# Fetching and splitting a stage's first operands in the stage before: a five-stage expert kernel on one core

## What is computed

```python
def L0_cond(x, t):                      # 1 shared and 8 routed experts, top 2
    shared = (silu(x @ sw1.T) * (x @ sw3.T)) @ sw2.T
    s = sigmoid(x @ router_w.T + (t @ router_t_w.T)[:, None])
    combine = normalized gates of the top 2 of s + router_bias
    routed = sum_e combine[e] * (gelu(x @ rw1[e].T) @ rw2[e].T)
    return (shared + routed) / 3

def L0_ffn(h):                          # one of 8 experts for each batch
    sel = argmax(softmax(gelu(h[:, -1] @ Wp1 + bp1) @ Wp2 + bp2))
    z = gelu(h @ W1[sel] + b1[sel]) @ W2[sel] + b2[sel]
    return h + 0.3 * (z @ Wo + bo)

def L1_cond(x, token_ids, first):       # 16 experts by a hash of the token id
    d = shift(x, first) - x             # the token before, in each batch
    y = sum over a token's expert of relu(xk @ w_key[e])**2 @ w_value[e]     # xk = x + d * maa_k
    return sigmoid((x + d * maa_r) @ w_recept) * y

def L1_ffn(x):                          # a recurrence over the 32 batches, state c: 128 x 512
    for xt in x:
        f, i = sigmoid(xt @ wf.T + c @ uf.T + bf), sigmoid(xt @ wi.T + c @ ui.T + bi)
        c = f * c + i * tanh(xt @ wc.T + c @ uc.T + bc)
    return tanh(x @ wo.T + c @ uo.T + bo)

x = x + L0_ffn(L0_cond(x, cond))
x = x + L1_ffn(L1_cond(x, token_ids, cond))
```

## Time and profile before

| | |
|---|---|
| runs of the kernel before | 2596.1 us median of 3 (2594.2 to 2601.7) |
| the profiled execution | 2597.6 us, span 2595.9 us |
| instructions | 40713 |
| mean granted clock of PE | 0.98 |
| busy, share of the span | PE 95%, PE weight loads 79%, DVE 44%, ACT 35%, POOL 21% |
| read from and written to device memory | 541.9 and 161.6 MB |

### The profile page before, as it was taken

One profiled execution on the slowest core, in us unless ns is written; L12 is line 12 of the kernel. 1 busy time (PEld: TensorE's weight loads), 2 busy tenths in 40 slices (PEclk: granted clock), 3 DMA queues, 4 the chain that ended last, 5 costly groups with the idle time before them and its releaser, 6 DMA issues. The chain is left out here.

```text
span 2595.9 us, 40713 instructions
## 1 busy us (share of the span) xinstructions
PE 2476.0 (95%) x12551; PEld 2058.9 (79%) x12553; DVE 1141.7 (44%) x1746; ACT 900.9 (35%) x1451; POOL 555.3 (21%) x498
## 2 busy tenths in 40 slices
PE   8999999998999599999999969999969999999999
PEld 4788888877888488888888859999958888888876
DVE  4655455432333144343434336666733323332356
ACT  2333333324555222222222236666632222222233
POOL 1100000002222166657656520000001111111000
PEclk9999999998999799999999989999989999999999
DMA  7699898877444643364344246666631111111035
GB/s 289 219 329 324 296 335 306 316 281 277 141 142 145 245 155 114 114 239 128 105 152 148 89 180 245 224 238 223 242 132 33 33 28 28 33 33 29 19 105 170
DMA packets 137648, 446.60 MB, mean 172 GB/s; under 512 B 30578, under 2 KB 33074, under 8 KB 118368
## 3 DMA queue, kind: packets, MB, share of 16 engines
q1 hardware_dynamic: 109904, 342.78, 37.5%
q0 software_dynamic: 18736, 60.80, 7.7%
q10 hardware_dynamic: 8928, 41.98, 4.2%
HBM read 541.93 MB, written 161.58 MB: 271 GB/s over the span
## 5 line engine op out<-in xcount | busy, mean ns | idle before, releaser
L93 PE MATMUL s_g<-wx_hi,s_x_hi 128*128 128x512 f32 x512 | 206.7, 404 | 6.6 <-DVE s_x_lo L1931 4.0
L95 PE MATMUL s_g<-wx_hi,s_x_lo 128*128 128x512 f32 x512 | 201.8, 394 | 0.0
L94 PE MATMUL s_g<-wx_lo,s_x_hi 128*128 128x512 f32 x512 | 201.2, 393 | 0.0
L1665 DVE TENSOR_TENSOR s_w_lo<-s_w_raw,s_w_hi 128x1024 fp32r<-128x1024 f32 x128 | 151.0, 1222 | 68.0 <-ACT s_w_hi L1617 66.4
L93 PE MATMUL s_g<-s_w_hi,s_c_hi 128*128 128x512 f32 x384 | 152.4, 397 | 0.0
L93 PE MATMUL s_h_ps<-s_x_hi,s_w_hi 128*128 128x256 f32 x512 | 145.8, 285 | 6.4 <-DVE s_w_lo L1665 6.4
L95 PE MATMUL s_g<-s_w_hi,s_c_lo 128*128 128x512 f32 x384 | 149.8, 390 | 0.0
L94 PE MATMUL s_g<-s_w_lo,s_c_hi 128*128 128x512 f32 x384 | 149.4, 389 | 0.0
L95 PE MATMUL s_h_ps<-s_x_hi,s_w_lo 128*128 128x256 f32 x512 | 145.6, 284 | 0.0
L94 PE MATMUL s_h_ps<-s_x_lo,s_w_hi 128*128 128x256 f32 x512 | 145.6, 284 | 0.0
L1832 POOL DMA_INDIRECT s_y<-mid_hash_out,s_rec x32 | 31.4, 982 | 484.9 <-DMA s_rec<-mid_rec 480.1
(11 more groups left out here) (355 smaller groups left out, 6850.3 us busy)
## 6 DMA issues: line engine op xcount, KB each, us to landing
s_half<-mid_w ACTq DMA_DIRECT2D x128, 2048.0 KB
s_w_raw<-in_w SPq DMA_DIRECT2D x64, 512.0 KB, 6.1
mid_w<-s_x_grp SPq DMA_DIRECT2D x32, 1024.0 KB, 5.3
mid_w<-s_pool_b SPq DMA_DIRECT2D x32, 1024.0 KB, 4.9
s_w_raw<-in_w1h SPq DMA_DIRECT2D x16, 2048.0 KB, 8.3
s_w_raw<-in_w2h SPq DMA_DIRECT2D x16, 2048.0 KB, 7.5
mid_routed<-s_o_sb SPq DMA_DIRECT2D x72, 256.0 KB, 2.4
s_w<-mid_rw SPq DMA_DIRECT2D x8, 2048.0 KB, 19.8
```

The lines of the kernel that those rows point to most:

```text
L93: pe.matmul(out, a_hi, w_hi, start=first, stop=False, skip_group_check=True)
L94: pe.matmul(out, a_hi, w_lo, start=False, stop=False, skip_group_check=True)
L95: return pe.matmul(out, a_lo, w_hi, start=False, stop=last, skip_group_check=True)
L1665: dve.tensor_tensor(lo[:, c], raw[:, c], hi[:, c], ALU.subtract).then_inc(S[name + "_lo"], 1)
```

## The change

At all four places where a stage follows another, something that the later one needs first is fetched, or fetched and split, in the earlier one:

- Stage 1 no longer splits rw in parts. SP loads experts 0 to 4 raw, 1 MB each, into the place of their low halves; ACT writes the high halves (`routed_hi`), DVE overwrites the raw with the low. DVE gets twelve small operations in `places`, which note at which of the tiles 40, 48, 56, 64 and 72 the experts 3 and 5 are done (`unused_by`).
- Stage 2 loads experts 5 to 7 raw and splits them in tiles 2 to 7 (`late_hi`, `late_lo`). At tile 36 SP loads what stage 4's first batch needs; at each of the five tiles named, `load_first` loads the first w1 and w2 into `half` under a condition. It doesn't wait for its last output stores; POOL does in stage 4.
- Stage 4 loads and splits stage 5's first w1 (`load_hashed`, `hashed_hi`, `hashed_lo`), does the last batch's `mix` on DVE (`last_mix`), and leaves its last stores to stage 5.
- Stage 5 loads, in its last expert, the state weights, the first state and the first rows of stage 6, and splits the first two (`unit_hi`, `unit_lo`, `turn_state`, `state_hi`, `state_lo`).
- Stage 6 starts with the state products of batch 0 (`first_c_part`) and leaves them out of the pipeline.

Buffers move to other places so that what is loaded ahead doesn't meet what is still used. The core of the diff:

```diff
 stage_shared
-        PARTS = [("rw", 0), ("rw", 1)] + [(w, k) for w in ("w1", "w2") for k in range(DC)]
+        PARTS = [(w, k) for w in ("w1", "w2") for k in range(DC)]
...
             for e in range(EARLY):
-                row = sp.value_load(keep["order"][0:1, 0, e:e + 1], min_val=0, max_val=ER - 1)
-                sp.dma_start(keep["w"][:, bass.ds(row, 1)].bitcast(FP32),
-                             d["rw"][bass.ds(row, 1)].rearrange("o p l s n -> p o l s n")).then_inc(S[f"rw_in{e}"], 16)
+                sp.dma_start(keep["w_raw"][e][:, :, 1], raw_experts[:, e]).then_inc(S[f"rw_in{e}"], 16)
...
+            def routed_hi(e):
+                act.wait_ge(S["gu"], G * HC)
+                act.wait_ge(S[f"rw_in{e}"], 16)
+                act.activation(keep["w"][:, e, :, 0], keep["w_raw"][e][:, :, 1], ACT.Copy).then_inc(S["rw_hi"], 1)
             def o_out(g):
                 for m in range(TG):
+                    if g == G - 1:
+                        routed_hi(m)
+                        if m == TG - 1:
+                            routed_hi(EARLY - 1)
...
+                for n, last_expert in enumerate((3, 5)):
+                    for k, tiles in enumerate(CHECKED):
+                        op(dve.tensor_scalar(reached[:, n, k:k + 1], end[0:1, last_expert:last_expert + 1], float(tiles),
+                                             None, ALU.is_le))
...
+            for e in range(EARLY):
+                dve.wait_ge(S["rw_hi"], e + 1)
+                dve.tensor_tensor(keep["w"][:, e, :, 1], keep["w_raw"][e][:, :, 1], keep["w"][:, e, :, 0],
+                                  ALU.subtract)
 stage_routed
             for e in range(EARLY, ER):
+                sp.dma_start(w_raw[e][:, :, 1], raw_experts[:, e]).then_inc(S[f"w_in{e}"], 16)
...
+                if i == CHECKED[0] - 4:
+                    sp.wait_ge(S["ordered"], 1)
+                    for dst, src in (("bo", "bo"), ("maa_k", "maa_k"), ("maa_r", "maa_r")):
+                        sp.dma_start(keep["s4_" + dst][:], ins[src].partition_broadcast(P)).then_inc(S["s4_params_in"], 16)
...
+                if i + 1 in CHECKED:
+                    for layer in range(2):
+                        load_first(layer, CHECKED.index(i + 1))
...
+            def load_first(layer, n):
+
+                unused = sp.value_load(keep["unused_by"][0:1, layer, n:n + 1], min_val=0, max_val=1) > 0
+                e = sp.value_load(order[0:1, 0, 0:1], min_val=0, max_val=ER - 1)
+                s = sp.value_load(table[0:1, layer, 0:1], min_val=0, max_val=NW - 1)
+                sp.wait_ge(S["mm2"], CHECKED[n])
+                for k, name in enumerate((("s4_w1_in0", "s4_w1_in1"), ("s4_w2_in00", "s4_w2_in10"))[layer]):
+                    sp.dma_start(half[:, bass.ds(s, 1), 2 * k:2 * k + 2].bitcast(FP32),
+                                 d["w"][bass.ds(2 * e + 2 + layer, 1), :, 2 * k:2 * k + 2].rearrange("o p k s n -> p o k s n"),
+                                 cond=unused).then_inc(S[name], 16)
             straight(RT, [(0, store), (0, load)])
-            for n in range(NI):
-                sp.wait_ge(S[f"o_out{n}"], 16 * RT // NI)
...
+            def late_hi(i):
+                n = i - LATE_AT
+                if 0 <= n < len(LATE):
+                    e, layer = LATE[n]
+                    act.wait_ge(S[f"w_in{e}"], 16)
+                    act.activation(w[:, e, layer, 0], w_raw[e][:, layer, 1], ACT.Copy).then_inc(S["w_hi"], 1)
...
-            straight(RT, [(2, gelu), (1, x_hi_), (3, o_copy), (2, h_hi), (3, wo_hi), (0, choose)])
+            straight(RT, [(2, gelu), (1, x_hi_), (3, o_copy), (2, h_hi), (0, late_hi), (3, wo_hi), (0, choose)])
 stage_ffn
+            def load_hashed(i, n, turn):
+                if isinstance(i, int) and i == NB - 1:
+                    sp.wait_ge(S["mm2"], NB)
+                    sp.dma_start(keep["w1_raw"][:], ins["w1h"][0]).then_inc(S["hashed_in"], 16)
...
             sp.wait_ge(S["x1_out"], 16 * NB)
-            sp.wait_ge(S["r_out"], 16 * NB)
...
             def gather(i, n, turn):
+                if isinstance(i, int) and i == 0:
+                    for m in range(4):
+                        pool.wait_ge(R[f"o_out{m}"], 16 * RT // 4)
...
+            def hashed_hi(i, n, turn):
+                if isinstance(i, int) and i == NB - 1:
+                    act.wait_ge(S["hashed_in"], 16)
+                    for c in range(DC):
+                        act.activation(keep["w1_hi"][:, c], keep["w1_raw"][:, c], ACT.Copy).then_inc(S["hashed_hi"], 1)
...
-                (1, h_lo(0)), (2, x1_), (1, h_lo(1)), (3, part_lo(xr_lo, tz_ps, xr_hi, "xr_hi", "xr_lo")),
+                (1, h_lo(0)), (2, x1_), (1, h_lo(1)), (3, last_mix),
+                (3, part_lo(xr_lo, tz_ps, xr_hi, "xr_hi", "xr_lo")), (3, hashed_lo),
 stage_hashed
+            def load_ahead(e):
+                if isinstance(e, int) and e == EH - 1:
+                    sp.wait_ge(F["r_out"], 16 * NB)
+                    sp.dma_start(staged[:], ins["gate_w"][0:NST].rearrange("u p n -> p u n")).then_inc(S["u_in"], 16)
+                    sp.dma_start(first_rec[:], d["rec"][0]).then_inc(S["rec_in"], 16)
+                    for m in range(2):
+                        sp.wait_ge(S[f"tx{m}"], EH)
+                    sp.dma_start(first_c[:], ins["in_c"].partition_broadcast(P)).then_inc(S["c_in"], 16)
+                    sp.dma_start(first_r[:], d["r"][0]).then_inc(S["r_in"], 16)
...
+                (2, g_hi), (2, out(1)), (1, w2(0, 2)), (1, relu(0)), (1, w2(2, 3)), (1, relu(1)), (1, h_hi(0)), (1, w2(3, 4)),
+                (1, unit_hi(0, 1)), (1, relu(2)), (1, h_hi(1)), (1, unit_hi(1, 2)), (1, relu(3)), (1, h_hi(2)),
+                (1, h_hi(3)), (1, unit_hi(2, 4)), (1, state_hi), (1, unit_hi(4, UNITS)), (0, x_hi_(0)), (0, x_hi_(1)),
+                (0, w1(0, 4)), (1, out(0))])
 stage_recurrent
+            def first_c_part():
+                for g in range(NG):
+                    for k in range(DC):
+                        product(pe, g_ps[0][g][:], (c_hi[:, k], c_lo[:, k]), (state_w(0, g, k), state_w(1, g, k)),
+                                k == 0, False)
...
             def c_part(i, n, turn):
-                pe.wait_ge(S["c_lo"], i + 1)
+                if isinstance(i, int) and i == 0:
+                    return
...
-            turn_c(0)
+            first_c_part()
```

More of the change, by code:

```diff
@@ L32 @@
 AHEAD_BYTES = 4 * D * 4
+UNITS = 6
+STATE_BYTES = (2 * D + 2 * UNITS * HS + 2 * D + D) * 4
 EPS = 1e-9
@@ new lines, in stage_ffn @@
+        keep["w1_lo"], keep["w1_hi"], keep["w1_raw"] = ahead("w1_lo", 1), ahead("w1_hi", 2), ahead("w1_raw", 3, FP32)
+        right = lambda n, s, t=FP32: ctx.enter_context(nc.sbuf_tensor("s4_" + n, s, t, side="right"))
+        right("half", [P, HALF_BYTES // 4])
+        half = keep["half"]
+        r = right("r", [P, D])
+        y_hi = right("y_hi", [P, DC, P], FP32R)
+        y_lo = right("y_lo", [P, DC, P], FP32R)
+        h_pre = right("h_pre", [P, 2, D])
+        h = right("h", [P, 2, D])
@@ new lines, in stage_ffn @@
+        ht_hi = right("ht_hi", [P, HC, P], FP32R)
+        ht_lo = right("ht_lo", [P, HC, P], FP32R)
+        z = right("z", [P, D])
+        z_hi = right("z_hi", [P, DC, P], FP32R)
+        z_lo = right("z_lo", [P, DC, P], FP32R)
+        b1 = right("b1", [P, HS])
+        b2 = right("b2", [P, D])
+        base = right("base", [P, 2, D])
+        y_part = right("y_part", [P, D])
+        right("first", [P, (CHOICE_BYTES + FIRST_BYTES) // 4])
+        shared, bo, maa_k, maa_r = (keep["s4_" + n] for n in ("shared", "bo", "maa_k", "maa_r"))
@@ L1648, in stage, with unit_hi, state_hi @@
                     wait_for(act, S[f"o_out{m}"], e * 16)
-                    act.activation(o_sb[:, m], o_ps[m][:], ACT.Copy).then_inc(S[f"o_ready{m}"], 1)
+                    act.activation(o_sb[m][:], o_ps[m][:], ACT.Copy).then_inc(S[f"o_ready{m}"], 1)
                 return stage
+            def unit_hi(first, end):
+                def stage(e):
+                    if isinstance(e, int) and e == EH - 1:
+                        for n in range(first, end):
+                            if n < 2:
+                                act.wait_ge(S["u_in"], 16)
+                                act.wait_ge(S["w1_lo"], (EH - done["w1"]) * DC)
+                            else:
+                                act.wait_ge(S["h_ps"], EH * NQ)
+                            if n >= NST:
+                                act.wait_ge(S["u_again_in"], 16)
+                            act.activation(u[:, n, 0], staged[:, n % NST], ACT.Copy).then_inc(S["u_hi"], 1)
+                return stage
+            def state_hi(e):
+                if isinstance(e, int) and e == EH - 1:
+                    act.wait_ge(S["c_turned"], 1)
+                    act.wait_ge(S["h_ps"], EH * NQ)
+                    act.activation(keep["c_hi"][:], tx_ps[0][:], ACT.Copy).then_inc(S["c_hi"], 1)
```

(14 more changed lines are left out.)

367 lines of the change are left out of this document (209 added, 158 removed).

## The result

The changed kernel takes 2584.5 us (median of 7 runs, 2580.9 to 2587.3) against 2598.3 us (median of 7, 2594.2 to 2601.7): a ratio of 0.9942, 95% interval 0.9931 to 0.9953, so 0.6% faster. The direction was forecast, the size was not: 14 us instead of 41, outside the range of 2536 to 2574 us. The profiled execution has a span of 2579.9 us, 16.0 less than the 2595.9 of before.

What follows compares the result with a forecast made beforehand. TensorE, busy 95% of the span, was taken as the bound, so only its standstills and the half clock after them could be won. Terms summed to 40.6 us: 2597.6 to 2557.0, stated as 2556 against the median, range 2536 to 2574.

Steps and rivals of the forecast that it cites:

- Stage 1: Stage 1: twelve small VectorE operations ahead of the scan delay the product that frees gate bank 0, -1.7 us.
- Seam 1 to 2: Between stages 1 and 2: TensorE restarts 0.5 us after VectorE's last subtraction, near 582.7, +1.0 us.
- Stage 2: Stage 2: late expert splits -2.4 us, stall at tile 4 gone +9.8, load burst after tile 39 stalling tile 44 -14.3.
- Seam 2 to 4: Between stages 2 and 4: uncrowded gathers let TensorE start at 883.0 instead of 890.56, +7.5 us.
- Stage 4: Stage 4, second tile: weight loads already in place, so all but about 1 us of its 9.2 us stall goes, +10.1 us.
- Seam 4 to 5: Between stages 4 and 5: weights split beforehand and x loaded first, products at 1523.7 instead of 1535.87, +12.2 us.
- Seam 5 to 6: Between stages 5 and 6: state products start early, x products come at 1923.0 instead of 1932.74, +9.7 us.
- what follows: Stage 6 after first x products: 36 products no longer follow +7.8 us, no long half clock +2.9, second split uncovered -2.0.
- A: Rival, stage 2: output stores are not held by the burst, so the 14.3 us stay in hand, 2541 us; chance 0.18.
- C: Rival, stage 2: conditionally skipped loads still move their bytes, four further checks stall, 57 us lost, 2613 us; chance 0.03.
- B: Rival, stages 1, 2 and 5: moved splits are not covered, costing 3, 4.5 and 6.6 us more, 2570 us; chance 0.16.
- D: Rival, seam 2 to 4: slots busy until the last check, so the change doesn't reach it, 2559 us; chance 0.02.

## Why the prediction was right and wrong

**Stage 1 (-1.7, measured +1.0).** The term was right: a wait of 1.9 us for the gate bank appeared, and fell to 0.2 without nine of the twelve operations. What was missing is a gain: the down products start 0.2290 instead of 0.2333 us apart, 768 x 0.0043 = 3.3 us. Their operands lie elsewhere in SBUF, at remainders of 384 and 320 instead of 480 and 256, and moving them again gave 0.2268; that the places made the gain was not tried in the kernel before.

**Seam 1 to 2 (+1.0, measured +1.2)** is right, by its mechanism too: VectorE's last subtraction ended at 581.7, 2.3 us behind ACT's last copy, and TensorE restarted at 582.0.

**Stage 2 (-6.9, measured -6.4)** is right in the sum and in its main step: the stall at tile 4 went and came back at tile 44, priced at 14.3 us and worth 15.6. ACT waited 15.3 us instead of "some 12". Two misses cancel, so the closeness is in part luck: the burst cost 1.3 us more than its term, and the late splits less than their 2.4. From one tile's transposes to the next's, the tiles with splits take 3.53 to 3.75 us, against 3.54 and 3.55 before, which is 0.6 us in all.

**Seam 2 to 4 (+7.5, measured +4.5): mis-sized.** The path is the predicted one: the last check with its six register reads keeps SP, the engines meet, the gathers start. Its terms were too small. SP was through 6.6 us after the last product (881.5 against 874.9) where 6.0 were put down, and the restart took 1.2 us instead of 0.5, so the first gather started after 7.8 us instead of 6.5. The second gather landed 5.4 us after issue (883.95 to 889.36), not 3.5; why was not tried.

**Stage 4 (+10.1, measured -2.0): the largest miss, 12 us.** The step that failed is "Those loads are now in place: all but about 1 us goes". In place were the first expert's. The second batch has a new expert, and its w1 is issued behind the first Gelu in both kernels (900.62 and 900.75); the stall for y merely stood ahead of it. The prediction never asked when that load lands, though it had asked what is late next elsewhere. Issued earlier, it gives back 8.1 us. Stage 4 then gains 6.1 over before; of the 4 us that still lack, the products with Wo and the receptance hold 768 x 0.0012 = 0.9 (0.2336 us apart instead of 0.2324), and the other 3 lie within what this stage varies.

**Seam 4 to 5 (+12.2, measured +12.2)** is right: the first product comes 8.8 us after stage 4's last.

**Stage 5 (no term, measured -5.9).** "Buffers move to other places" stood in the description of the change and got no price. One place, 320 bytes, costs 4.5 us (768 x 0.0059); moving it back gives 5.5 us of the kernel's time, moving it in the kernel before costs 5.9. With it moved back, stage 5 lacks 0.9 us, which is the last expert with its unit splits; the prediction had 1.0 for them, but counted it in the +9.7 of the next seam.

**Seam 5 to 6 (+9.7, measured +7.2) and what follows (+8.7, measured +4.1): right in mechanism but for the clock, mis-sized.** The stage opens with the 36 products 2.0 us after the last product, the second tile's split shows its gap (2.2 us where 2.0 was put down). But the first gather "3.5 us or, beside the bias loads, 5" took 8.4, and x came 3.2 us behind the state products. "The gap is too short for a long half clock" failed with it: behind TensorE's waits of 3.2 and 2.1 us, 5.2 us ran at 1.2 GHz, so 2.6 of the +2.9 were not gained. The other 1.8 us lie in the step of the recurrence: 17.32 us against 17.26, over 30 steps. Runs with the same code in this stage have 17.28 and 17.32; its cause is open.

**The rivals.** A (stores not held) is out by ACT's 15.3 us. C (skipped loads move their bytes) is out because no later check is followed by such a wait, and the queues move 413.0 MB with one check as with five. B (splits uncovered) did not come: no wait of TensorE for a split in the tails of stages 1 and 5 is over 0.5 us. D is out since the burst ran at tile 40. The time was lost mostly in two places for reasons that no rival names: a load in stage 4 that stands behind an event of the first tile, and the place of a tensor in stage 5. Nor did the signs by which the prediction would call itself wrong come (the burst's stall absent or twice as long, a tail waiting for a split): they watched the feared steps, not the gains taken for granted.

## What to carry to other kernels

When a prefetch removes a stage's first stall, follow the second tile with the same care: the next load may stand behind an event of the first tile and be hidden only by the stall that goes. Bytes that are fetched ahead belong on a queue in portions that the latest store behind them can bear, and conditional transfers at the end of a stage cost their issue and reads at the seam even when they move nothing (15.7 us against 10.8 here). A change that moves buffers is worth a look at the spacing of matmuls in stretches without waits, before and after: here two such shifts were worth some 3 and 5 us with opposite signs.
